# The last batch of an attention-and-experts layer: VectorE sums the fourth tile's experts, ScalarE scales the last expert, the output leaves in three pieces

## The chip, the cores and the metric

The kernel runs on one core of one Trainium2 chip. Its time is device microseconds, start to end of one execution. The engines are TensorE (PE, its weight loads PEld), VectorE (DVE), ScalarE (ACT), GpSimd (POOL) and SyncE (SP), which only issues transfers here.

## What is computed

The input x is 8 x 512 x 128. It is normalised to xn, and the output is x plus an attention of xn plus a mixture of 8 experts of which each token takes its best two. Masked scores are set to 0, not to minus infinity.

```
def attention(x, Wq, Wk, Wv):            # per batch, T = 512, width 128
    q, k, v = x @ Wq.T, x @ Wk.T, x @ Wv.T
    attn = (q @ k.T) * tril(ones(T, T))
    return softmax(attn / sqrt(T)) @ v

def experts(x, Wg, We, be):              # E = 8, tokens t
    gates = softmax(x @ Wg)
    top_g, top_i = top_k(gates, 2); top_g /= sum(top_g)
    dispatch[e, t] = top_g where e in top_i[t], else 0
    return sum_e dispatch[e, t] * (x[t] @ We[e] + be[e])

xn = layernorm(x)
out = x + attention(xn, Wq, Wk, Wv) + experts(xn, Wg, We, be)
```

## The kernel before

The 512 tokens of a batch are four tiles of 128. The batches 0 to 7 go through a pipeline that is written out by hand: each engine has one list of calls, in program order, and semaphores order the engines against each other. An engine does its calls in the order written, so a call that waits holds all that stand behind it. The last batch, B - 1 = 7, and the end of batch 6 have lists of their own, behind the loop.

TensorE, for each tile t of batch b:

- `wide(b, k, t)` multiplies xn by a group of weights: C (values, expert 7, gate logits; 264 columns), A (four experts, 512 columns) and B (three experts, 384 columns). Each is three matmuls, of a high and a low part (L239, L240, L243), into one of four PSUM banks, the ring. `ring_free` lets it start only when the use of the group four places before it in the list of groups is over. In the last batch these are: B0 waits for A3 of batch 6, A1 for `sv_rows`, A2 for ScalarE's scaling of A0, B2 for the mix of tile 0, B3 for the scaling of A1, A3 for the mix of tile 1, and the row transpose DT for the scaling of A2.
- `scores(b, t)` writes the scores of the tile (t + 1) * 128 columns wide to one of three banks; `transpose_probs(b, t)` (L277) turns the exponentials, t + 1 blocks; `attend(b, t)` (L293) multiplies them with the values into the bank attb, 2 (t + 1) matmul records in the trace.
- `value_sums` (SV) and `transpose_rows` (DT, L328) prepare one low-rank matmul, `bias` (L334), which adds the masked keys' part and the experts' biases to all four tiles of attb. It ends the batch on TensorE.

VectorE: the gate (maxima, sum, reciprocal, `gate_out`, L528), `sv_rows` (L608), the masking of scores with their maximum (`mask_scores`, L560) and its negation `negate_max` (nmx, L567), `mix_b(b, t, i)` (L543), which adds gate times expert for the three experts of group B to x, the softmax sums (`softmax_sum`, `softmax_tot`, `softmax_rec`), and `finish_tile(b, t)` (L597), which scales attb and adds ffn into o_s.

ScalarE: copies out of PSUM, `softmax_exp` (L840), `probs_copy` (L855), and `scale_experts(b, t)` (L829), four multiplications of group A's experts by their gates into ysc. `rows_copy` (L886) lies between DT and the bias.

GpSimd: `scale_last(b)` (L1003) multiplies expert 7 of all four tiles by its gate, into y7. `sum_experts(b, t)` (L1010 to L1017) is a chain of four additions: the four scaled experts, y7, and the mix, into ffn. `bias_rows(b)` (L1029 to L1041) builds the rows for DT out of the gates and softmax totals.

SyncE stores batches 0 to 6 whole. The last batch goes in two pieces: tiles 0 to 2 when they are finished, then tile 3.

## Time and profile before

| | us |
|---|---|
| median of 3 runs | 132.51 (130.95 to 132.6) |
| the profiled execution's own time | 132.71 |
| its span in the profile | 130.69 |
| TensorE busy | 121.3 |
| VectorE / ScalarE / GpSimd busy | 102.1 / 101.4 / 96.2 |

The span is what the trace shows, from the first to the last event; 2.0 us lie around it. All times of the trace are counted from the start of the span. A busy TensorE is not TensorE at its peak, since matmuls overlap: in a timeline the record of one lasts longer than the step to the next. The start times in the chain of work are the better measure of what one costs.

### The profile page before, as it was taken

The numbers are of one execution on the slowest core, as the hardware profiler recorded it, in microseconds if no ns is written. First come the engines' busy times: TensorE is split into PE (matmuls) and PEld (weight loads), VectorE is DVE, ScalarE is ACT, GpSimd is POOL, SyncE is SP. The second block draws the span as 40 slices with busy tenths as digits, with TensorE's granted clock in tenths as the row PEclk, the third lists the DMA queues.
The fourth block names the chain that finished last, engine by engine and source line by source line (L and its number), as shares of the span: only waits on it lengthen the run. The fifth ranks groups of instructions, "written<-read, shape, count | busy, mean of one in ns | idle before, by whom it ended". The sixth has DMA issues, their size and how long they took to land.

```text
span 130.7 us, 3014 instructions
## 1 busy us (share of the span) xinstructions
PE 121.3 (93%) x766; PEld 109.1 (83%) x766; DVE 102.1 (78%) x507; ACT 101.4 (78%) x341; POOL 96.2 (74%) x216
## 2 busy tenths in 40 slices
PE   4839999999999999999999999999999999999870
PEld 4717878998989989999899999999899899888650
DVE  0477789797988799697969796979877985967822
ACT  2145699979986999789996999699869999656850
POOL 7080228669995998689967997799859986788881
PEclk9999999999999999999999999999999999999999
DMA  2996000000020002000200020000200020002002
GB/s 65 362 295 164 0 0 8 0 3 3 10 70 5 3 0 80 0 0 3 82 3 3 0 78 10 0 0 7 78 5 0 0 80 0 0 5 83 3 0 80
DMA packets 8929, 5.18 MB, mean 40 GB/s; under 512 B 328, under 2 KB 8784, under 8 KB 8912
## 3 DMA queue, kind: packets, MB, share of 16 engines
q1 hardware_dynamic: 8608, 4.79, 12.5%
q10 hardware_dynamic: 304, 0.20, 0.5%
q8 instruction: 6, 0.10, 0.3%
q14 instruction: 11, 0.09, 0.2%
HBM read 2.89 MB, written 2.10 MB: 38 GB/s over the span
## 4 chain that ended last, share of the span: by engine, by line
PE 83%; DVE 7%; DMA 3%; POOL 2%; ACT 1%; issue 1%; POOLq 0%
PE ring L239 13%; PE ring L240 13%; PE ring L243 13%; PE attb L293 12%; PE score L277 6%; PE ring L320 4%; PE score L243 4%; PE score L240 4%; PE score L239 3%; DMA x_all<-in_x_dram 3%; PE ring L302 2%; PE ring L310 2%; PE ring L313 2%; PE ring L311 2%; DVE xn L648 2%; PE ring L328 1%
## 5 line engine op out<-in xcount | busy, mean ns | idle before, releaser
L829 ACT ACTIVATE ysc<-ring,gate 128x128 f32<-128x128 f32 x128 | 36.4, 372 | 3.4 <-DVE gate L528 1.5
L239 PE MATMUL ring<-w_hi,xT_hi 128*128 128x264 f32 (+2 forms) x96 | 35.2, 367 | 0.6 <-DVE mix L543 0.4
L240 PE MATMUL ring<-w_lo,xT_hi 128*128 128x264 f32 (+2 forms) x96 | 33.0, 344 | 0.0
L243 PE MATMUL ring<-w_hi,xT_lo 128*128 128x264 f32 (+2 forms) x96 | 32.9, 343 | 0.0
L1010 POOL TENSOR_TENSOR ysc<-ysc 128x256 f32<-128x256 f32 x32 | 23.5, 734 | 7.3 <-ACT ysc L829 7.3
L293 PE MATMUL attb<-c_s,probT 128*128 128x128 f32 x160 | 23.3, 278 | 0.0
L543 DVE SCALAR_TENSOR_TENSOR mix<-ring,gate,mix 128x128 f32<-128x128 f32 x64 | 22.0, 344 | 0.2
L239 PEld LDWEIGHTS ring<-w_hi,xT_hi 128*128 128x128 f32 x96 | 18.7, 194 | 3.3 <-DVE mix L543 0.6
L293 PEld LDWEIGHTS attb<-c_s,probT 128*128 128x128 f32 x160 | 20.8, 191 | 0.4
L240 PEld LDWEIGHTS ring<-w_lo,xT_hi 128*128 128x128 f32 x96 | 18.6, 194 | 1.6
L243 PEld LDWEIGHTS ring<-w_hi,xT_lo 128*128 128x128 f32 x96 | 18.5, 193 | 1.4
L1017 POOL TENSOR_TENSOR ffn<-ysc,mix 128x128 f32<-128x128 f32 x32 | 14.6, 457 | 6.5 <-DVE tot L582 4.3
L840 ACT ACTIVATE prob<-score,nmx 128x128 f32<-128x128 f32 (+3 forms) x32 | 17.4, 542 | 0.6 <-DVE nmx L567 0.6
L543 DVE SCALAR_TENSOR_TENSOR mix<-ring,gate,x_all 128x128 f32<-128x128 f32 x32 | 11.0, 345 | 7.9 <-PE ring L243 7.7
L597 DVE SCALAR_TENSOR_TENSOR o_s<-attb,rinv,ffn 128x128 f32<-128x128 f32 x32 | 10.8, 344 | 8.0 <-PE attb L334 7.9
L1013 POOL TENSOR_TENSOR ysc<-ysc,y 128x128 f32<-128x128 f32 x32 | 14.7, 461 | 2.5
L1011 POOL TENSOR_TENSOR ysc<-ysc 128x128 f32<-128x128 f32 x32 | 14.7, 459 | 2.5
L560 DVE CUSTOM_DVE_ANT_0 score<-score,causal 128x128 f32<-128x128 f32 (+3 forms) x32 | 15.7, 490 | 0.1
L990 POOL TENSOR_TENSOR rstd<-veps,half 128x4 f32<-128x4 f32 x8 | 8.1, 1014 | 9.5 <-DVE veps L475 5.9
L277 PE MATMUL score<-ident,prob 128*128 128x128 f32 x80 | 14.2, 276 | 0.2 <-ACT prob L840 0.2
L855 ACT COPY probT<-score 128x128 f32<-128x128 f32 (+3 forms) x32 | 13.8, 430 | 0.4 <-PE score L277 0.3
L801 ACT ACTIVATE xn<-x_all,nmr,rstd 128x128 f32<-128x128 f32 x29 | 12.0, 483 | 1.6 <-POOL nmr L998 1.6
(99 smaller groups left out, 248.9 us busy)
## 6 DMA issues: line engine op xcount, KB each, us to landing
x_all<-in_x_dram SPq DMA_DIRECT2D x8, 256.0 KB, 5.9
out_dram<-o_s SPq DMA_DIRECT2D x7, 256.0 KB, 2.3
w_f<-in_w_stacked_dram SPq DMA_DIRECT2D x1, 580.0 KB, 5.2
out_dram<-o_s SPq DMA_DIRECT2D x1, 192.0 KB, 2.1
wqk_s<-in_w_attention_dram ACTq DMA_DIRECT2D x1, 128.0 KB, 3.7
shapes_s<-in_shapes_dram ACTq DMA_DIRECT2D x1, 64.5 KB
out_dram<-o_s SPq DMA_DIRECT2D x1, 64.0 KB, 1.8
be_s<-in_be_dram ACTq DMA_DIRECT2D x1, 4.0 KB
```

Of the source, the lines that this page charges most:

```text
L239: nc.tensor.matmul(dst, hi, w_h, start=True, stop=False)
L240: nc.tensor.matmul(dst, hi, w_l, start=False, stop=False)
L243: return nc.tensor.matmul(dst, lo, w_h, start=False, stop=True)
L277: last = nc.tensor.transpose(score_bank(b, t)[:, c], prob[:, t, c], ident[:])
L293: last = nc.tensor.matmul(attb[:, t * P:(t + 1) * P], probT[:, b % 2, t, j * P:(j + 1) * P], c_s[:, b % 2, j, 0:P], start=(t == 0), stop=F ...
L543: ins = nc.vector.scalar_tensor_tensor(mix[:, t, i, :], bank(f"B{t}", b)[:, i * P:(i + 1) * P], gate[:, b % 2, t, 4 + i:5 + i], before, AL ...
L560: cnt["maxed", b, t] = chain.mark(nc.vector.tensor_tensor_reduce(score_bank(b, t)[:, 0:n], score_bank(b, t)[:, 0:n], causal[:, (NT - 1 - t ...
L829: last = nc.scalar.mul(ysc[:, t, e, :], bank(f"A{t}", b)[:, e * P:(e + 1) * P], gate[:, b % 2, t, e:e + 1])
L840: nc.scalar.activation(prob[:, t, 0:n], score_bank(b, t)[:, 0:n], ACT.Exp, bias=nmx[:, b % 2, t:t + 1], scale=1.0, accum_out=rs[:, b % 2, ...
L1010: chain.step(nc.gpsimd.tensor_tensor(y[:, 0:2, :], y[:, 0:2, :], y[:, 2:4, :], ALU.add))
L1011: chain.step(nc.gpsimd.tensor_tensor(y[:, 0, :], y[:, 0, :], y[:, 1, :], ALU.add))
L1013: chain.step(nc.gpsimd.tensor_tensor(y[:, 0, :], y[:, 0, :], y7[:, b % 2, t, :], ALU.add))
```

## The change

Only the end of batch 6 and the last batch are touched; the loops before are the same.

- `scale_last(B - 1)` on GpSimd is replaced by `scale_last_act(B - 1)` on ScalarE: three multiplications, for tiles 0 to 2.
- `scale_experts(B - 1, 3)` on ScalarE and `sum_experts(B - 1, 3)` on GpSimd go. VectorE does the same sum for tile 3 in a chain: four `mix_a` read group A's experts straight from PSUM, `mix_last` adds expert 7, and `finish_last` takes the place of `finish_tile(B - 1, 3)`.
- The orders of the calls on TensorE, VectorE, ScalarE and GpSimd are rewritten.
- The last batch is stored in three pieces: tiles 0 and 1, tile 3, tile 2. The finishes come in the order 0, 1, 3, 2.

```diff
@@ SyncE
+            b = B - 1
+            sp.wait_ge(S["fin_done"], b * NT + 2)
+            sp.dma_start(out_v[b][:, 0:2, :], o_s[:, b % 2, 0:2, :]).then_inc(S[f"stored{b % 2}"], 16)
+            for n, t in enumerate((3, 2)):
+                sp.wait_ge(S["fin_done"], b * NT + 3 + n)
+                sp.dma_start(out_v[b][:, t, :], o_s[:, b % 2, t, :]).then_inc(S["stored_last"], 16)
+            sp.wait_ge(S["stored_last"], 32)
@@ TensorE
             transpose_probs(B - 1, 0)
+            scores(B - 1, 2)
             wide(B - 1, "B", 0)
-            scores(B - 1, 2)
             wide(B - 1, "A", 1)
+            scores(B - 1, 3)
             wide(B - 1, "B", 1)
-            scores(B - 1, 3)
+            transpose_probs(B - 1, 1)
             wide(B - 1, "A", 2)
             wide(B - 1, "B", 2)
+            transpose_probs(B - 1, 2)
+            attend(B - 1, 0)
             wide(B - 1, "B", 3)
-            transpose_probs(B - 1, 1)
-            wide(B - 1, "A", 3)
-            attend(B - 1, 0)
-            transpose_probs(B - 1, 2)
             transpose_probs(B - 1, 3)
             attend(B - 1, 1)
+            wide(B - 1, "A", 3)
             attend(B - 1, 2)
@@ VectorE
+            def mix_a(e):
+                b, t = B - 1, NT - 1
+                if e == 0:
+                    dve.wait_ge(S["wide_done"], wide_count("A", b, t))
+                    dve.wait_ge(S["mix_ready"], b * NT + t + 1)
+                else:
+                    chain.need(cnt["mix_a", e - 1])
+                cnt["mix_a", e] = chain.mark(nc.vector.scalar_tensor_tensor(
+                    mix[:, t, e % 2, :], bank(f"A{t}", b)[:, e * P:(e + 1) * P], gate[:, b % 2, t, e:e + 1],
+                    mix[:, t, 2 if e == 0 else 1 - e % 2, :], ALU.mult, ALU.add))
+
+            def mix_last():
+                b, t = B - 1, NT - 1
+                chain.need(cnt["mix_a", 3])
+                cnt["mix_last"] = chain.mark(nc.vector.scalar_tensor_tensor(
+                    mix[:, t, 0, :], c_s[:, b % 2, t, Y_AT:Y_AT + P], gate[:, b % 2, t, 7:8], mix[:, t, 1, :], ALU.mult, ALU.add))
+
+            def finish_last(b):
+                t = NT - 1
+                chain.need(cnt["mix_last"])
+                nc.vector.scalar_tensor_tensor(o_s[:, b % 2, t, :], attb[:, t * P:(t + 1) * P], rinv[:, b % 2, t:t + 1],
+                                               mix[:, t, 0, :], ALU.mult, ALU.add).then_inc(S["fin_done"], 1)
...
             negate_max(B - 1, 1)
+            gate_out(B - 1)
             finish_tile(B - 2, 0)
-            gate_out(B - 1)
...
+            for e in range(4):
+                mix_a(e)
+            mix_last()
             finish_tile(B - 1, 0)
             finish_tile(B - 1, 1)
+            finish_last(B - 1)
             finish_tile(B - 1, 2)
-            finish_tile(B - 1, 3)
@@ ScalarE
+            def scale_last_act(b):
+                act.wait_ge(S["gate_ready"], b + 1)
+                act.wait_ge(S["ffn_ready"], (b - 2) * NT + NT)
+                for t in range(NT - 1):
+                    last = nc.scalar.mul(y7[:, b % 2, t, :], c_s[:, b % 2, t, Y_AT:Y_AT + P], gate[:, b % 2, t, 7:8])
+                last.then_inc(S["y7_ready"], 1)
...
             sv_high(B - 1)
+            scale_last_act(B - 1)
+            softmax_exp(B - 1, 1)
+            probs_copy(B - 1, 0)
             scale_experts(B - 1, 0)
-            probs_copy(B - 1, 0)
-            softmax_exp(B - 1, 1)
+            softmax_exp(B - 1, 2)
             scale_experts(B - 1, 1)
-            scale_experts(B - 1, 2)
             probs_copy(B - 1, 1)
-            softmax_exp(B - 1, 2)
             masked_exp(B - 1)
             softmax_exp(B - 1, 3)
             probs_copy(B - 1, 2)
+            scale_experts(B - 1, 2)
             probs_copy(B - 1, 3)
-            scale_experts(B - 1, 3)
@@ GpSimd
             sum_experts(B - 2, 3)
-            scale_last(B - 1)
             sum_experts(B - 1, 0)
             sum_experts(B - 1, 1)
+            bias_rows(B - 1)
             sum_experts(B - 1, 2)
-            bias_rows(B - 1)
-            sum_experts(B - 1, 3)
```

Three places show the new order. Line numbers below 540 on TensorE move by one and those of VectorE by one or 27, since functions are added.

VectorE at the last gate, before. grec is the reciprocal of the gate sums, nmx the negated maximum of tile 1, the o_s rows are the finishes of batch 6, the rhs_rows are `sv_rows`.

```order
L517 RECIPROCAL grec<-gsum 128x4
L543 SCALAR_TENSOR_TENSOR mix<-ring3,gate,mix 128x128
L567 TENSOR_SCALAR nmx<-mx 128x1
L597 SCALAR_TENSOR_TENSOR o_s<-attb,rinv,ffn 128x128
L528 TENSOR_TENSOR gate<-gexp,grec 128x32
L608 SCALAR_TENSOR_TENSOR rhs_rows<-sv_hi,shapes_s,ring1 3x128 x3
L543 SCALAR_TENSOR_TENSOR mix<-ring0,gate,x_all 128x128
L597 SCALAR_TENSOR_TENSOR o_s<-attb,rinv,ffn 128x128 x2
L543 SCALAR_TENSOR_TENSOR mix<-ring0,gate,mix 128x128
L597 SCALAR_TENSOR_TENSOR o_s<-attb,rinv,ffn 128x128
```

The same place now; L587 with 128x384 is the mask of tile 2.

```order
L518 RECIPROCAL grec<-gsum 128x4
L544 SCALAR_TENSOR_TENSOR mix<-ring3,gate,mix 128x128
L594 TENSOR_SCALAR nmx<-mx 128x1
L529 TENSOR_TENSOR gate<-gexp,grec 128x32
L624 SCALAR_TENSOR_TENSOR o_s<-attb,rinv,ffn 128x128
L635 SCALAR_TENSOR_TENSOR rhs_rows<-sv_hi,shapes_s,ring1 3x128 x3
L624 SCALAR_TENSOR_TENSOR o_s<-attb,rinv,ffn 128x128
L587 ISA score0,mx<-score0,causal 128x384
L587 ISA mx 128x1
L624 SCALAR_TENSOR_TENSOR o_s<-attb,rinv,ffn 128x128
L594 TENSOR_SCALAR nmx<-mx 128x1
L624 SCALAR_TENSOR_TENSOR o_s<-attb,rinv,ffn 128x128
```

The gate has passed the first finish of batch 6, and the mask of tile 2 has passed the mixes of tile 0.

TensorE around group A3 of the last batch (bank ring2, 512 columns), before. score2, score0 and score1 hold tiles 1, 2 and 3; the attb rows are `attend`.

```order
L277 MATMUL score2<-ident,prob 128x128 x2
L239 MATMUL ring2<-w_hi,xT_hi 128x512
L240 MATMUL ring2<-w_lo,xT_hi 128x512
L243 MATMUL ring2<-w_hi,xT_lo 128x512
L293 MATMUL attb<-c_s,probT 128x128
L277 MATMUL score0<-ident,prob 128x128 x3
L277 MATMUL score1<-ident,prob 128x128 x4
L293 MATMUL attb<-c_s,probT 128x128 x9
```

The same place now; ring1 with 384 columns is group B3.

```order
L278 MATMUL score0<-ident,prob 128x128 x3
L294 MATMUL attb<-c_s,probT 128x128
L240 MATMUL ring1<-w_hi,xT_hi 128x384
L241 MATMUL ring1<-w_lo,xT_hi 128x384
L244 MATMUL ring1<-w_hi,xT_lo 128x384
L278 MATMUL score1<-ident,prob 128x128 x4
L294 MATMUL attb<-c_s,probT 128x128 x2
L240 MATMUL ring2<-w_hi,xT_hi 128x512
L241 MATMUL ring2<-w_lo,xT_hi 128x512
L244 MATMUL ring2<-w_hi,xT_lo 128x512
L294 MATMUL attb<-c_s,probT 128x128 x7
```

All transposes and two of the `attend` calls now stand ahead of A3, seven matmuls of `attend` behind it.

VectorE at the end, before: the softmax totals of the last batch, the mixes of tile 3 (ring1) and the four finishes.

```order
L582 TENSOR_TENSOR tot<-tot,rs 128x4
L586 RECIPROCAL rinv<-tot 128x4
L543 SCALAR_TENSOR_TENSOR mix<-ring1,gate,mix 128x128 x2
L597 SCALAR_TENSOR_TENSOR o_s<-attb,rinv,ffn 128x128 x4
```

The end now: L559 is `mix_a`, L567 `mix_last`, L574 `finish_last`.

```order
L609 TENSOR_TENSOR tot<-tot,rs 128x4
L544 SCALAR_TENSOR_TENSOR mix<-ring1,gate,x_all 128x128
L613 RECIPROCAL rinv<-tot 128x4
L544 SCALAR_TENSOR_TENSOR mix<-ring1,gate,mix 128x128 x2
L559 SCALAR_TENSOR_TENSOR mix<-ring2,gate,mix 128x128 x4
L567 SCALAR_TENSOR_TENSOR mix<-c_s,gate,mix 128x128
L624 SCALAR_TENSOR_TENSOR o_s<-attb,rinv,ffn 128x128 x2
L574 SCALAR_TENSOR_TENSOR o_s<-attb,rinv,mix 128x128
L624 SCALAR_TENSOR_TENSOR o_s<-attb,rinv,ffn 128x128
```

Five chained instructions have come in ahead of the finishes, and tile 3's finish stands third.

## Rows read from the trace of the kernel before

**Rows 1.** The page: busy time by engine; a group: busy us, mean ns of one | idle before.

```profile
PE 121.3 (93%) x766; PEld 109.1 (83%) x766; DVE 102.1 (78%) x507; ACT 101.4 (78%) x341; POOL 96.2 (74%) x216
...
L855 ACT COPY probT<-score 128x128 f32<-128x128 f32 (+3 forms) x32 | 13.8, 430 | 0.4 <-PE score L277 0.3
```

**Rows 2.** The chain in order of time, last batch: start us, us, what.

```profile
115.39 0.23 PE ring L239
...
118.14 0.17 PE ring L239
...
118.66 0.23 PE score L239
...
119.35 0.23 PE ring L239
...
120.05 0.17 PE ring L239
...
122.56 0.79 ACT prob L840 x2
```

**Rows 3.** Timeline of TensorE: start us, us, engine, line, what, [idle before <-releaser].

```profile
121.72 0.50 PE L239 MATMUL ring<-w_hi,xT_hi 128*128 128x512 f32 x1 [0.40 <-DVE mix L543]
...
123.88 2.17 PE L293 MATMUL attb<-c_s,probT 128*128 128x128 f32 x18
```

**Rows 4.** Timeline of VectorE.

```profile
113.93 0.18 DVE L517 RECIPROCAL grec<-gsum 128x4 f32<-128x4 f32 x1
...
115.43 0.35 DVE L597 SCALAR_TENSOR_TENSOR o_s<-attb,rinv,ffn 128x128 f32<-128x128 f32 x1 [1.02 <-PE attb L334]
115.70 0.46 DVE L528 TENSOR_TENSOR gate<-gexp,grec 128x32 f32<-128x32 f32 x1
116.08 1.05 DVE L608 SCALAR_TENSOR_TENSOR rhs_rows<-sv_hi,shapes_s,ring 3x128 fp32r<-3x128 f32 x3
...
119.22 0.56 DVE L560 CUSTOM_DVE_ANT_0 score<-score,causal 128x384 f32<-128x384 f32 x1
...
120.94 0.73 DVE L543 SCALAR_TENSOR_TENSOR mix<-ring,gate,mix 128x128 f32<-128x128 f32 x2
121.58 0.69 DVE L560 CUSTOM_DVE_ANT_0 score<-score,causal 128x512 f32<-128x512 f32 x1
...
127.12 0.87 DVE L597 SCALAR_TENSOR_TENSOR o_s<-attb,rinv,ffn 128x128 f32<-128x128 f32 x3 [2.25 <-PE attb L334]
128.15 0.35 DVE L597 SCALAR_TENSOR_TENSOR o_s<-attb,rinv,ffn 128x128 f32<-128x128 f32 x1 [0.15 <-POOL ffn L1017]
```

**Rows 5.** Timeline of ScalarE.

```profile
100.90 1.65 ACT L801 ACTIVATE xn<-x_all,nmr,rstd 128x128 f32<-128x128 f32 x4 [0.18 <-POOL nmr L998]
...
116.22 1.14 ACT L829 ACTIVATE ysc<-ring,gate 128x128 f32<-128x128 f32 x4 [1.48 <-DVE gate L528]
```

**Rows 6.** Timeline of GpSimd.

```profile
115.65 0.45 POOL L1017 TENSOR_TENSOR ffn<-ysc,mix 128x128 f32<-128x128 f32 x1
116.23 1.05 POOL L1003 TENSOR_TENSOR y<-c_s,gate 128x512 f32<-128x512 f32 x1
...
124.51 0.23 POOL L1029 TENSOR_TENSOR gate_tot<-gate,tot 128x32 f32<-128x32 f32 x1
...
125.30 0.25 POOL L1041 TENSOR_TENSOR lhs_rows<-gate_tot,lhs_rows 128x32 fp32r<-128x32 f32 x1
125.78 0.72 POOL L1010 TENSOR_TENSOR ysc<-ysc 128x256 f32<-128x256 f32 x1 [0.23 <-ACT ysc L829]
...
127.66 0.45 POOL L1017 TENSOR_TENSOR ffn<-ysc,mix 128x128 f32<-128x128 f32 x1
```

**Rows 7.** Timeline of SyncE's queue: the two stores of the last batch.

```profile
128.02 0.37 SPq L214 DMA_DIRECT2D out_dram<-o_s  x1
128.52 0.40 SPq L216 DMA_DIRECT2D out_dram<-o_s  x1
```

More of the change, by code:

```diff
@@ L210, in _ @@
                 store(b)
-            b, t = B - 1, NT - 1
-            sp.wait_ge(S["fin_done"], b * NT + t)
-            sp.dma_start(out_v[b][:, 0:t, :], o_s[:, b % 2, 0:t, :]).then_inc(S[f"stored{b % 2}"], 16)
-            sp.wait_ge(S["fin_done"], b * NT + NT)
-            sp.dma_start(out_v[b][:, t, :], o_s[:, b % 2, t, :]).then_inc(S["stored_last"], 16)
-            sp.wait_ge(S["stored_last"], 16)
+            b = B - 1
[5 more added lines that the diff above has]
+            sp.wait_ge(S["stored_last"], 32)
             for i in range(2):
@@ L759, in _ @@
             sv_rows(B - 1, 2)
+            finish_tile(B - 2, 1)
+            mask_scores(B - 1, 2)
+            finish_tile(B - 2, 2)
+            negate_max(B - 1, 2)
+            finish_tile(B - 2, 3)
             mix_b(B - 1, 0, 0)
-            finish_tile(B - 2, 1)
-            finish_tile(B - 2, 2)
             mix_b(B - 1, 0, 1)
-            finish_tile(B - 2, 3)
+            mix_b(B - 1, 0, 2)
+            mask_scores(B - 1, 3)
             mix_b(B - 1, 1, 0)
-            mix_b(B - 1, 0, 2)
-            mask_scores(B - 1, 2)
+            negate_max(B - 1, 3)
+            mix_b(B - 1, 1, 1)
             mix_b(B - 1, 2, 0)
-            negate_max(B - 1, 2)
-            mix_b(B - 1, 1, 1)
             mix_b(B - 1, 1, 2)
-            mask_scores(B - 1, 3)
-            negate_max(B - 1, 3)
-            mix_b(B - 1, 3, 0)
             mix_b(B - 1, 2, 1)
@@ L778, in _ @@
             softmax_tot(B - 1)
+            mix_b(B - 1, 3, 0)
             softmax_rec(B - 1)
```

## The prediction

> **What bounds the kernel now.** I read the page first: TensorE is busy 93% of the span, 121.3 us [rows 1]. That is an average over eight batches, and the change touches only the last one, so the views that decide are the chain and the timelines from 115 us on. Nothing is moved ahead of the last gate, about 114.3 us, so the first 114 us should repeat.
>
> In the chain [rows 2], take the differences of the start times: `wide(B)` 384 columns costs 0.52 us (118.14 to 118.66), `scores` of tile 3 0.69, `wide(A)` 0.70. The tail of attention, 18 multiplications in 2.17 us [rows 3], gives (2.17 - 0.27)/17 = 0.11 us for each 128-column one; probability transposes go at the same pace. TensorE's work between the end of the bias of batch 6 (115.39, where A0 begins, [rows 2]) and the end of the last `attend` (123.88 + 2.17 = 126.05, [rows 3]) is then 4 x 0.70 + 4 x 0.52 + 0.52 + 0.69 + 10 x 0.11 + 20 x 0.11 = 9.4 us; I carry 9.45, since the steps are rounded, and the dates below add to that. The stretch lasts 10.66. So **TensorE stands still for 1.2 us** there; the largest piece is A3 (121.72), which waits 0.40 for VectorE's mix of tile 1 [rows 3]. The chain shows why: VectorE's mix waits for B2, the mask of tile 3 (0.69 us) comes behind it at 121.58, and ScalarE's exponential of tile 3 only at 122.56 [rows 2, 4].
>
> After TensorE comes a fixed tail: row transpose, copy, bias, and the first `finish_tile` at 127.12, that is 1.07 us behind the last `attend`; then four finishes, the last held until 128.15 by GpSimd's `ffn` of tile 3 (done 127.66 + 0.45), and the last store issued at 128.52 [rows 3, 4, 6, 7]. The span ends 130.69 - 128.52 = 2.17 us later.
>
> **The change part by part.**
>
> *Gate ahead of finish_tile(6,0).* The reciprocal of the gate sum ends at 114.11, but the gate stood behind a finish that waited 1.02 us for TensorE, and came out at 115.70 + 0.46 = 116.16 [rows 4]. Now it can start at about 114.4 and takes 0.18 (its median in the other batches) to 0.46 us: ready at 114.6 to 114.9, 1.3 to 1.5 us earlier. ScalarE waited 1.48 us for exactly this [rows 5]. Its own new waits are for things of batch 5 and 6 that are long done. The three `sv_rows` start right behind the finish, 115.70 instead of 116.08, and so end at 116.78: A1, at 117.27 in the new flow, does not wait for them.
>
> *GpSimd loses `scale_last` (1.05 us) and `sum_experts(7,3)` (125.78 to 128.11, 2.33 us) [rows 6].* ScalarE gains three multiplications that read SBUF. The nearest rows are xn from SBUF, four in 1.65 us, about 0.40 each in a row [rows 5], and ysc from PSUM, four in 1.14, about 0.26 each. So 0.8 to 1.2 us; I take 1.2, since SBUF is the source. They run 114.64 to 115.84, in time in which ScalarE waited; the exponential of tile 1 (at most the 0.79 of tile 3, [rows 2]) ends by 116.6, and TensorE asks for it only at 119.20. It loses one `scale_experts` (1.14). Cost on the path: nothing; were the cover gone, 1.2 us.
>
> *VectorE gains four chained `mix_a` and one `mix_last`.* A pair of chained mixes takes 0.73 [rows 4], 0.36 each: 4 x 0.36 = 1.45. `mix_last` reads two SBUF tensors. The row to look at is the gate at 115.70: 0.46 us instead of 0.18, ending at 116.16, just behind GpSimd's `ffn` (115.65 + 0.45 = 116.10) [rows 4, 6]. So it costs 0.35 alone and up to 0.35 + 0.45 = 0.80 beside GpSimd; I take 0.8, since `sum_experts(7,2)` runs then. [...]
>
> *The new order, followed through.* TensorE from 115.39, no stalls: A0 to 116.10, transpose 0 to 116.21, scores 2 to 116.74, B0 to 117.27, A1 to 117.97, scores 3 to 118.67, B1 to 119.20, transposes 1 to 119.42, A2 to 120.12, B2 to 120.65, transposes 2 to 120.98, attend 0 to 121.20, B3 to 121.73, transposes 3 to 122.17, attend 1 to 122.61, A3 to 123.31, attend 2 to 123.98, attend 3 to 124.85. VectorE: sv_rows to 116.78, finish 1, mask 2 from 117.04 (0.56, [rows 4]), finish 2, negate (nmx 2 at 117.91), finish 3, mix 0 from 118.10 to 119.16, mask 3 from 119.09 to 119.84 with its read-out, nmx 3 at 120.1 instead of just ahead of 122.56, then mix 1 and mix 2 interleaved: mix 1 ready at 121.30, behind the first part of mix 2, which waits for B2 (120.65). ScalarE: scale 0 116.44 to 117.55, exp 2 from 117.94 to 118.7 at most, scale 1 to 119.6, copy 1 to 119.9, exp 3 from 120.15 to 120.9 (0.79 with the read-out of its sum, [rows 2]), copies by the mean of 0.43 [rows 1] and tile 3's somewhat longer: copy 2 from 121.0 to 121.5, scale 2 to 122.5, copy 3 from 122.4 to 123.0.
>
> Each wait of TensorE against its date: B2 needs mix 0 (119.18 for 120.12), A3 needs mix 1 (121.30 for 122.61), transposes 3 need exp 3 (120.9 for 121.73), attend 3 needs copy 3 (123.0 for 123.98), the row transpose needs `rows_ready`. For that GpSimd waits for tot: exp 3 at 120.9, then VectorE's softmax_sum and softmax_tot at about 122.3 with both delayed by GpSimd; the five operations of `bias_rows` take 124.51 to 125.55, 1.04 us [rows 6], so 123.35 for 124.85. The smallest slack is **0.8 us**. Then 1.2 us of stalls go, and the last `attend` ends at 124.85 instead of 126.05: **-1.20**.
>
> *The tail.* First finish 1.07 later, 125.91. VectorE must be done by then: A3 ends 123.31, mix_a 123.42 to 124.87, mix_last to 125.65 at the dear end: 0.25 us in hand. `sum_experts(7,2)` starts at 123.5 and takes 2.33: 125.83, wanted at 126.69 by the last finish. The finishes start every 0.26 us (three in 0.87, [rows 4]): 125.91, 126.17, 126.43 (tile 3), 126.69 (tile 2). The three pieces queue on SP: the first is issued when tile 1 ends, 126.55; an issue takes 0.37 and 0.40 in [rows 7], and I put 0.05 between two (at most the 0.13 between those): second 126.97, third 127.42. Its data (tile 2, done 127.04) is ready by then, so SP's own queue is what comes last. Before, the last issue began 1.40 behind the first finish (127.12 to 128.52), now 1.51: **+0.11**. The last piece is again 64 KB, so I keep 2.17 us from issue to the end.
>
> Sum: -1.20 + 0.11 = **-1.1 us**; span 129.6. The profiled execution took 132.71, so 131.6; it lies 0.2 above the median of 132.51, and against that median I get **131.4 us**.
>
> **Rivals.**
> 1. *A wait comes back at about half price.* Slacks are 0.8 to 1.5 us, but VectorE is in order and the chain mix 0, B2, mix 2, mix 1, A3 goes twice between engines; and mix_last has 0.25 us in hand. For: two of these slacks rest on what VectorE does in a row. Against: 0.8 us is more than the roundings of the steps on the way. A stall of 0.3 to 0.7: 131.9.
> 2. *Gains beyond the sum.* The third piece could be issued as soon as its tile is done (127.07, 0.35 earlier) if issues overlap, and the end could hang on a smaller queue. The issues of [rows 7] do not overlap, which speaks against it: 131.0.
> 3. *The end was set by GpSimd and the stores, and stays.* Then only 0.15 us of the wait for `ffn` goes and the 0.11 comes: 132.4. The chain runs through GpSimd at the end [rows 6], but TensorE's bias comes only 1 us before, so both ends move.
> 4. *Slower: VectorE becomes the bound at the end.* Place: A3, four chained mix_a, mix_last, then finish_tile(7,0) behind them. A3 begins 0.9 later than before (121.72, now 122.61), and 1.45 + 0.8 + 0.1 us of VectorE work that used to be ScalarE's and GpSimd's stands in front of all the finishes. The price is one for one from the moment that A3 ends later than 123.55; the gain is gone when it ends later than 124.65, which a wait for mix 1 would do if that came at 123.95 instead of 121.30. At 0.5 us beyond: 133.0. Against: 2.6 us of slip is more than any engine in this stretch shows.
> 5. *mix_last waits for GpSimd's chain, not for one instruction of it.* The instructions of `sum_experts(7,2)` follow each other closely, its last ends at 125.83. Had mix_last to wait for all of them, it would end at 126.2, and the first finish would slip from 125.91 by 0.3: 131.7. Against: the gate at 115.70 waited out one `ffn` only.
>
> **How the numbers follow.** All stalls gone and tail as summed: 0.55, 131.1 to 131.8 by profile to median. Rival 1: 0.2. Rival 2: 0.08. Rival 3: 0.07. Rival 4: 0.05. Rival 5: 0.05. The three times of before spread from 130.95 to 132.6, so a median of after can sit 1.5 us lower than the sum by that alone, or 0.3 higher; low end 131.4 - 1.5 = 129.9, high end rival 3 and part of rival 4, 132.7. Two per cent of 132.51 is 2.65 us, about what a measurement of this kernel can tell from no change; faster by more than that needs 129.86 or less, which only a spread as that of before gives: 0.06. Slower by over 2%, 135.2, needs rival 4 at five times its price: 0.02. Within: 0.92.
>
> **What the new profile would show.** Right: gate at about 114.6 and no 1.48 us of idle ScalarE before the first scale; nmx of tile 3 near 120.1; no wait before A3 and transposes 3; last attend near 124.9; first finish near 125.9; three issues one after the other from 126.5; span 129.6. Wrong: A3 or B2 with an idle time that ends with VectorE; the first finish released by VectorE's own mix and not by the bias; the last store waiting for a finish; a later issue than 127.5. The forecast falls if the old stalls reappear at the new places of the transposes, or if the last 64 KB land more slowly behind two fresh pieces.

## The result, and the profile after

| | before | changed |
|---|---|---|
| median of 20 runs, us | 132.64 (130.95 to 133.32) | 131.39 (130.34 to 132.03) |
| ratio, with 95% interval | | 0.9929 (0.9899 to 0.9958) |
| profiled execution: time, span, us | 132.71, 130.69 | 131.18, 129.11 |

The kernel became faster by 0.7%, and the interval of the ratio leaves 1 out; by ratio that is 0.9 us, by medians 1.25. The ratios here and below leave out executions that took over 1.5% more than the fastest of the same kernel: that is four of the six of experiment e1, whose ratio so rests on two, and one of e8, the very one that was profiled.

The two profiled spans differ by 1.58 us, but not all of this is the change. The stream of instructions is the same up to the last gate, and yet batch 6's bias ends at 115.39 before and at 115.02 in the changed kernel. In a second profile of the very same changed kernel (experiment e12) it ends at 115.56. So I count every date behind that point, called T0 below, from it. Behind T0 the span takes 15.30 us before and 14.10 in both profiles of the changed kernel: **the change is worth 1.20 us there**.

The stretch table of the changed kernel, T0 to the end of the last `attend`, and from there to the end (columns: the stretch, its length, busy us and instructions of PE, PEld, DVE, ACT, POOL, granted clock, DMA share, GB/s):

The first row is the same stretch before; a row of the changed kernel for each of the two follows.

```profile
115.39:126.05 10.66, 10.11 (x61) 8.51 (x60) 7.99 (x29) 7.91 (x27) 9.18 (x21) 1.00 0.09 28
...
115.02:124.44 9.42, 9.42 (x61) 8.50 (x60) 8.83 (x32) 6.86 (x24) 7.02 (x17) 1.00 0.11 31
124.44:129.10 4.66, 0.58 (x3) 0.19 (x1) 1.77 (x6) 0.27 (x1) 0.91 (x2) 0.87 0.19 56
```

TensorE is busy in all of its 9.42 us, where the stretch took 10.66 before. By busy time it was idle for only 0.55 us of that, not 1.2: the record of a 512-column matmul lasts 0.39 us and the next starts 0.23 behind it, so the first part of every wait is covered by the record before it. The start times give the whole loss. Its timeline shows the places where the stalls used to be; a row without brackets at its end had no idle time ahead of it. It answers to [rows 3]:

```profile
121.14 0.60 PE L278 MATMUL score<-ident,prob 128*128 128x128 f32 x4
121.58 0.61 PE L294 MATMUL attb<-c_s,probT 128*128 128x128 f32 x4
121.95 0.48 PE L240 MATMUL ring<-w_hi,xT_hi 128*128 128x512 f32 x1
...
122.72 1.72 PE L294 MATMUL attb<-c_s,probT 128*128 128x128 f32 x14
124.28 0.27 PE L329 MATMUL ring<-ident,lhs_rows 128*128 128x128 f32 x1
125.00 0.47 PE L335 MATMUL attb<-rhs_rows,lhsT_rows 128*128 128x512 f32 x1 [0.45 <-ACT lhsT_rows L924]
```

VectorE, against [rows 4]: the gate ends at 114.19, ahead of T0; the negated maximum of tile 3 comes at 119.62, T0 + 4.6, where it was T0 + 7.0; then the new sum.

```profile
113.96 0.23 DVE L529 TENSOR_TENSOR gate<-gexp,grec 128x32 f32<-128x32 f32 x1
...
119.62 0.14 DVE L594 TENSOR_SCALAR nmx<-mx 128x1 f32<-128x1 f32 x1
...
123.08 1.51 DVE L559 SCALAR_TENSOR_TENSOR mix<-ring,gate,mix 128x128 f32<-128x128 f32 x4
124.62 0.50 DVE L567 SCALAR_TENSOR_TENSOR mix<-c_s,gate,mix 128x128 f32<-128x128 f32 x1
125.50 0.61 DVE L624 SCALAR_TENSOR_TENSOR o_s<-attb,rinv,ffn 128x128 f32<-128x128 f32 x2 [0.39 <-POOL ffn L1055]
126.03 0.34 DVE L574 SCALAR_TENSOR_TENSOR o_s<-attb,rinv,mix 128x128 f32<-128x128 f32 x1
126.29 0.34 DVE L624 SCALAR_TENSOR_TENSOR o_s<-attb,rinv,ffn 128x128 f32<-128x128 f32 x1
```

Here is a trap. The row at 125.50 names GpSimd's `ffn` as what ended VectorE's wait, and the chain of waits follows it back through GpSimd:

```profile
124.52 0.45 POOL ysc L1051
124.97 0.04 issue
125.01 0.51 POOLq L93
125.52 0.34 DVE o_s L624
```

But the first finish needs the bias (125.00 + 0.47 = 125.47) and the `ffn` of tile 0, which was long done. The `ffn` that ends at 125.51 is tile 2's, wanted by the last finish at 126.29. Two events came within 0.04 us, and the profile took the later. In e2's profile, where no edit touches this place, the same row names the bias. Which of them held the finish, experiment e9 decides.

GpSimd and SyncE, against [rows 6, 7]:

```profile
124.52 0.45 POOL L1051 TENSOR_TENSOR ysc<-ysc,y 128x128 f32<-128x128 f32 x1
125.05 0.46 POOL L1055 TENSOR_TENSOR ffn<-ysc,mix 128x128 f32<-128x128 f32 x1
```

```profile
126.14 0.37 SPq L214 DMA_DIRECT2D out_dram<-o_s  x1
126.56 0.96 SPq L217 DMA_DIRECT2D out_dram<-o_s  x2
```

The two issues from 126.56 take 0.47 and 0.45 us, so the last begins at 127.07, though its tile was done at 126.63.

### The profile page after: what moved, and what is told of

Read it like the earlier page. It is cut to its first block, busy times and chain, and to the rows that moved or that the text cites. A ratio compares the mean times of both kernels' runs of the same rounds, so it can differ in the third digit from the quotient of the medians.

```text
span 129.1 us, 3013 instructions
## 1 busy us (share of the span) xinstructions
PE 120.2 (93%) x766; PEld 108.9 (84%) x766; DVE 103.3 (80%) x512; ACT 101.1 (78%) x340; POOL 93.4 (72%) x211
## 4 chain that ended last, share of the span: by engine, by line
PE 84%; DVE 6%; DMA 3%; POOL 3%; issue 1%; POOLq 0%; DVEq 0%
PE ring L240 13%; PE ring L244 13%; PE ring L241 13%; PE attb L294 13%; PE score L278 6%; PE score L244 4%; PE score L241 4%; PE ring L321 4%; PE score L240 3%; DMA x_all<-in_x_dram 3%; PE ring L303 2%; PE ring L314 2%; PE ring L311 2%; PE ring L312 2%; PE ring L329 1%; PE attb L335 1%
## 5 line engine op out<-in xcount | busy, mean ns | idle before, releaser
L859 ACT ACTIVATE ysc<-ring,gate 128x128 f32<-128x128 f32 x124 | 35.4, 373 | 0.8 <-PE ring L244 0.3
L1048 POOL TENSOR_TENSOR ysc<-ysc 128x256 f32<-128x256 f32 x31 | 22.8, 735 | 8.4 <-ACT ysc L859 8.4
L587 DVE CUSTOM_DVE_ANT_0 score<-score,causal 128x128 f32<-128x128 f32 (+3 forms) x32 | 15.7, 491 | 0.7 <-PE score L244 0.6
```

The source lines that it names most:

```text
L587: cnt["maxed", b, t] = chain.mark(nc.vector.tensor_tensor_reduce(score_bank(b, t)[:, 0:n], score_bank(b, t)[:, 0:n], causal[:, (NT - 1 - t ...
L859: last = nc.scalar.mul(ysc[:, t, e, :], bank(f"A{t}", b)[:, e * P:(e + 1) * P], gate[:, b % 2, t, e:e + 1])
L1048: chain.step(nc.gpsimd.tensor_tensor(y[:, 0:2, :], y[:, 0:2, :], y[:, 2:4, :], ALU.add))
```

## The experiments

All are edits of the changed kernel, except e12, which is that kernel again. Each was run 6 to 12 times beside the kernel of before, whose median then was 132.34 to 132.42, and profiled once. Dates behind T0, us, from each kernel's profile:

| kernel | nmx, tile 3 | last attend ends | first finish starts | last finish ends | end of span | median | ratio to before (95%) |
|---|---|---|---|---|---|---|---|
| before | 7.0 | 10.66 | 11.73 | 13.11 | 15.30 | 132.64 | 1 |
| changed | 4.6 | 9.43 | 10.49 | 11.62 | 14.10 | 131.39 | 0.993 (0.990, 0.996) |
| e12, the same again | 4.6 | 9.43 | 10.50 | 11.62 | 14.10 | 131.20 | 0.990 (0.985, 0.994) |
| e1 gate late | 5.0 | 9.61 | 10.68 | 11.92 | 14.28 | 131.87 | 0.989 (0.981, 0.997) |
| e2 two pieces | 4.6 | 9.43 | 10.50 | 11.63 | 13.87 | 130.50 | 0.988 (0.983, 0.992) |
| e3 tile 3 back | 4.6 | 9.41 | 10.48 | 13.13 | 15.10 | 132.33 | 0.999 (0.996, 1.002) |
| e4 old TensorE order | 4.9 | 10.66 | 11.72 | 12.84 | 15.31 | 132.92 | 1.003 (1.001, 1.006) |
| e5 y7 on GpSimd | 4.6 | 9.43 | 10.50 | 11.62 | 14.10 | 131.17 | 0.991 (0.987, 0.995) |
| e6 three more mixes | 4.6 | 9.42 | 11.03 | 12.15 | 14.63 | 132.21 | 0.999 (0.996, 1.002) |
| e7 store from ScalarE | 4.6 | 9.44 | 10.50 | 11.63 | 13.83 | 131.44 | 0.992 (0.989, 0.996) |
| e8 old VectorE order | 7.1 | 13.51 | 14.58 | 15.70 | 18.19 | 134.22 | 1.012 (1.008, 1.017) |
| e9 rows early | 4.6 | 9.55 | 10.02 | 11.14 | 13.61 | 130.53 | 0.986 (0.982, 0.989) |
| e10 rows early, two pieces | 4.6 | 9.54 | 10.01 | 11.13 | 13.37 | 130.72 | 0.988 (0.984, 0.991) |
| e11 sum moved alone | 7.0 | 10.67 | 11.74 | 12.86 | 15.34 | 132.44 | 1.001 (0.998, 1.004) |

The dates repeat to 0.01 or 0.02 us from profile to profile wherever nothing was edited; the times of whole runs scatter by 1.5 us, since T0 itself does (113.5 to 115.9). Differences of 0.2 us are therefore read from the dates alone.

**e1: the gate back behind the finish.**

```diff
-            gate_out(B - 1)
             finish_tile(B - 2, 0)
+            gate_out(B - 1)
```

> The changed kernel, with the last gate put back behind the first finish of batch 6; all else as changed. Theory (TensorE is now without stalls, and the early gate is one of the reasons): counted from the end of batch 6's bias (T0, 115.02 in the changed kernel's trace), the gate comes at T0 + 0.8 instead of before T0, ScalarE's three y7 multiplications move from before T0 to after it, so the copy of tile 0's transposed probabilities comes at about T0 + 2.7 and holds scores 3 by 0.3, the exponential of tile 3 ends at about T0 + 6.3 instead of 5.5 and holds the transposes of tile 3 by about 0.2: the last attend ends at T0 + 9.9 instead of 9.42, time +0.5 us (0.3 to 0.8). Rival (the early gate only fills ScalarE's idle time; all slack is larger): same last attend at T0 + 9.4, time 0.

Measured: +0.18, between the 0.5 of the theory and the 0 of the rival. The gate came at T0 + 0.77 as expected, but only A1 waited, for the later `sv_rows`:

```profile
115.06 0.33 PE L244 MATMUL ring<-w_hi,xT_lo 128*128 128x384 f32 x1
115.32 0.50 PE L240 MATMUL ring<-w_hi,xT_hi 128*128 128x512 f32 x1
```

From the start of the last matmul of B0 to the first of A1 it is 0.26 us, and from there to the second of A1 0.34 (115.66); in the changed kernel it was 0.17 and 0.23. The two differences, 0.2 us together, are the loss, and the kernel of before has the same steps there, 0.27 and 0.33. The slacks on ScalarE held, so the 0.3 and 0.2 that I expected at scores 3 and the transposes of tile 3 were not lost. Off TensorE more was lost than shows at the end: GpSimd's `ffn` of tile 2 ended at T0 + 11.54 instead of 10.49 and held the last finish by 0.1 us (it ends at 11.92 instead of 11.62), which SP's queue of issues then covered. Of the 1.2 us the early gate is worth 0.2 by these dates; by medians it would be 0.5 and by ratios nothing, both within the scatter.

**e2: two pieces.**

```diff
-            for n, t in enumerate((3, 2)):
-                sp.wait_ge(S["fin_done"], b * NT + 3 + n)
-                sp.dma_start(out_v[b][:, t, :], ...).then_inc(S["stored_last"], 16)
-            sp.wait_ge(S["stored_last"], 32)
+            sp.wait_ge(S["fin_done"], b * NT + 4)
+            sp.dma_start(out_v[b][:, 2:4, :], ...).then_inc(S["stored_last"], 16)
+            sp.wait_ge(S["stored_last"], 16)
```

> The changed kernel with the last batch stored in two pieces, tiles 0 and 1, then tiles 2 and 3 together when all is finished. Theory (SP's own queue of issues, 0.37 to 0.47 us each, comes last; the third is issued at 127.06, 0.43 after the last finish at 126.63): the last issue comes 0.40 us sooner, 1.16 behind the first finish instead of 1.56, and the time falls by 0.3 to 0.4 us. Rival (128 KB at the end land later than 64 KB, or the issue overlaps with the landing of the earlier ones): 0, or slower by 0.1 to 0.3.

Measured: -0.23 behind T0. The timeline of SyncE's queue:

```profile
126.42 0.37 SPq L214 DMA_DIRECT2D out_dram<-o_s  x1
126.94 0.37 SPq L216 DMA_DIRECT2D out_dram<-o_s  x1
```

T0 is 115.28 in this profile, so the last issue comes at T0 + 11.66 instead of 12.05, the expected 0.4 sooner. From there to the end of the span it is 2.21 us instead of 2.04. Each theory has its part: the queue did come last, and 0.17 of it comes back in the landing. The third piece costs more than it brings.

**e3: tile 3 back on ScalarE and GpSimd**, all orders new.

```diff
-            for e in range(4):
-                mix_a(e)
-            mix_last()
             finish_tile(B - 1, 0)
             finish_tile(B - 1, 1)
-            finish_last(B - 1)
             finish_tile(B - 1, 2)
+            finish_tile(B - 1, 3)
@@ ScalarE
             probs_copy(B - 1, 3)
+            scale_experts(B - 1, 3)
@@ GpSimd
             sum_experts(B - 1, 2)
+            sum_experts(B - 1, 3)
```

> The changed kernel with the experts of tile 3 back on ScalarE (four multiplications behind the last copy, and a fourth y7) and GpSimd (a chain of additions behind that of tile 2), finishes in the order 0, 1, 2, 3 and pieces (0, 1), 2, 3; all orders else as changed. Theory (the reordering takes the stalls out of TensorE, but only with the sum on VectorE does the end follow): last attend stays at T0 + 9.4, GpSimd's chain of tile 3 starts when that of tile 2 ends (T0 + 10.5) and takes 2.33, so the last finish starts at T0 + 12.9 instead of 11.3 and the last issue at T0 + 13.2 instead of 12.04: time +1.2 us, nearly the time of before. Rival (the stalls are all there is to the gain): 0 to +0.2.

Measured: +1.00 behind T0, ratio 0.999. TensorE kept all it had won (9.41), and the end did not move: VectorE stood 1.44 us before the last finish, until GpSimd's chain was through.

```profile
126.13 0.87 DVE L624 SCALAR_TENSOR_TENSOR o_s<-attb,rinv,ffn 128x128 f32<-128x128 f32 x3 [2.54 <-POOL ffn L1053]
128.43 0.35 DVE L624 SCALAR_TENSOR_TENSOR o_s<-attb,rinv,ffn 128x128 f32<-128x128 f32 x1 [1.44 <-POOL ffn L1053]
```

```profile
126.08 0.72 POOL L1046 TENSOR_TENSOR ysc<-ysc 128x256 f32<-128x256 f32 x1
...
127.95 0.45 POOL L1053 TENSOR_TENSOR ffn<-ysc,mix 128x128 f32<-128x128 f32 x1
```

**e4: TensorE's old order**, the others new.

```diff
             wide(B - 1, "B", 0)
+            scores(B - 1, 2)
             wide(B - 1, "A", 1)
             wide(B - 1, "B", 1)
+            scores(B - 1, 3)
             wide(B - 1, "A", 2)
             wide(B - 1, "B", 2)
             wide(B - 1, "B", 3)
+            transpose_probs(B - 1, 1)
+            wide(B - 1, "A", 3)
             attend(B - 1, 0)
+            transpose_probs(B - 1, 2)
             transpose_probs(B - 1, 3)
...
```

> The changed kernel with TensorE's order of the last batch as before the change (tile 1's transposes behind group B3, A3 before the first attend, all other transposes behind A3); the other engines as changed. Theory (TensorE's order has to fit the others'): ScalarE's copy of tile 1 stands ahead of the exponential of tile 3 and now waits for transposes that come at T0 + 5.8, so the exponential ends at about T0 + 6.9 and the copy of tile 3 at T0 + 9.1; the last attend waits some 0.5 for it and ends at T0 + 9.9 to 10.1: +0.6 us (0.3 to 0.9). Rival (the gain comes from VectorE's order alone): 0.

Measured: last attend 10.66 instead of 9.9 to 10.1, +1.21 behind T0: the theory's mechanism, at twice the size. ScalarE's copy of tile 1 waits 1.25 us for its transposes, the exponential of tile 3 stands behind it, and the copy of tile 3 comes late:

```profile
121.04 0.37 ACT L893 COPY probT<-score 128x256 f32<-128x256 f32 x1 [1.25 <-PE score L278]
121.31 0.21 ACT L886 ACTIVATE em<-nmx 128x3 f32<-128x3 f32 x1
121.42 0.68 ACT L878 ACTIVATE prob<-score,nmx 128x512 f32<-128x512 f32 x1
...
122.72 0.48 ACT L893 COPY probT<-score 128x384 f32<-128x384 f32 x1 [0.53 <-PE score L278]
```

```profile
121.17 0.51 PE L240 MATMUL ring<-w_hi,xT_hi 128*128 128x512 f32 x1 [0.16 <-DVE mix L544]
...
124.77 1.16 PE L294 MATMUL attb<-c_s,probT 128*128 128x128 f32 x8 [0.54 <-ACT probT L893]
```

ScalarE waited another 0.53 us for tile 2's transposes with the scaling of tile 2 queued behind, which I had not counted. That this doubled the loss is an argument from these rows; no run parts the two waits.

**e5: expert 7 scaled on GpSimd.**

```diff
             sum_experts(B - 2, 3)
+            scale_last(B - 1)
             sum_experts(B - 1, 0)
@@ ScalarE
-            scale_last_act(B - 1)
```

> The changed kernel with expert 7 scaled by GpSimd again (one multiplication of four tiles, 1.05 us, ahead of sum_experts of tile 0), and no y7 on ScalarE. Theory (both engines have room there): GpSimd does it from about T0 + 0.7 to T0 + 1.8, before ScalarE has tile 0's experts scaled at T0 + 2.2, so nothing on TensorE's path moves: last attend T0 + 9.4, time 0 (within 0.15). Rival (ScalarE was freed for the exponentials by nothing else, or GpSimd's queue is what the change relieves): the sums of all tiles and the softmax rows come 1.05 us later, and the time rises by 0.3 or more.

Measured: every date the same to 0.01 us. This part of the change is worth nothing, as GpSimd had 1.5 us of idle time there.

**e6: three more chained mixes.**

```diff
             for e in range(4):
                 mix_a(e)
+            for e in range(3):
+                chain.need(cnt["mix_a", 3])
+                mix_a(3)
             mix_last()
```

> The changed kernel with the fourth mix of tile 3 done four times over instead of once, with the same result: three more chained VectorE instructions of 0.37 us in front of the finishes. Theory (VectorE has about 0.4 us in hand: mix_last ends at 125.12, the first finish starts at 125.50 when the bias comes): of the 1.1 us, 0.4 are swallowed, the first finish starts 0.7 later, released by VectorE's own mix and not by the bias, time +0.7 us (0.5 to 0.8). Rival (VectorE is already the bound at the end): +1.1. Rival (GpSimd's sum of tile 2, done at 125.51, is what held the first finish): +0.7 too, but then with the first finish never earlier than the end of that sum in any run.

Measured: first finish +0.54, end +0.53. VectorE's timeline:

```profile
123.92 2.67 DVE L559 SCALAR_TENSOR_TENSOR mix<-ring,gate,mix 128x128 f32<-128x128 f32 x7
126.62 0.35 DVE L567 SCALAR_TENSOR_TENSOR mix<-c_s,gate,mix 128x128 f32<-128x128 f32 x1
126.89 0.60 DVE L624 SCALAR_TENSOR_TENSOR o_s<-attb,rinv,ffn 128x128 f32<-128x128 f32 x2
```

Three more cost 2.67 - 1.51 = 1.16 us, and about 0.6 was swallowed. `mix_last` now runs when GpSimd has finished for good (at T0 + 10.48; T0 is 115.86 here, so 126.34) and takes 0.35 instead of 0.50; that is the 0.15 by which the expected 0.7 was too much. The first finish no longer waits for anything but the instruction ahead of it.

**e7: tile 3's piece from ScalarE's queue.**

```diff
@@ ScalarE
             rows_copy(B - 1)
+            act.wait_ge(S["fin_done"], (B - 1) * NT + 3)
+            act.dma_start(out_v[B - 1][:, 3, :], ...).then_inc(S["stored_last"], 16)
```

SP keeps tiles 0 and 1, and tile 2 when all four are finished.

> The changed kernel with tile 3's piece issued from ScalarE's queue, which is idle at the end, and the other two from SP. Theory (SP's queue of issues is what comes last): the last issue from SP comes at the last finish, 126.66 instead of 127.06, with 64 KB to land, so the time falls by 0.3 to 0.4 us; beside the two-piece kernel this tells what the size of the last piece is worth. Rival (issues from two queues hinder each other, or the landing and not the issue counts): 0.

Measured: -0.27 behind T0; the ratio, 0.992, cannot tell it from the changed kernel. The last issue comes 0.39 sooner, as in e2, and here too the end follows it by more, 2.17 us instead of 2.04. So it is not the size of the last piece (64 or 128 KB, 0.04 us apart) that gives back the 0.13 to 0.17.

**e8: VectorE's old order** of masks, mixes and finishes, from `sv_rows` to the last mix of tile 3, with the early gate and the new sum.

```diff
             sv_rows(B - 1, 2)
-            finish_tile(B - 2, 1)
-            mask_scores(B - 1, 2)
...
+            mix_b(B - 1, 0, 0)
+            finish_tile(B - 2, 1)
+            finish_tile(B - 2, 2)
+            mix_b(B - 1, 0, 1)
+            finish_tile(B - 2, 3)
+            mix_b(B - 1, 1, 0)
+            mix_b(B - 1, 0, 2)
+            mask_scores(B - 1, 2)
+            mix_b(B - 1, 2, 0)
+            negate_max(B - 1, 2)
...
+            mask_scores(B - 1, 3)
+            negate_max(B - 1, 3)
```

> The changed kernel with VectorE's order of masks, mixes and finishes of batch 6 and 7 as before the change, but the early gate and the new sum of tile 3 kept. Theory (the mask of tile 3 ahead of the mixes of tiles 1 and 2 is what frees the exponential of tile 3, and with it TensorE's transposes): the mask of tile 3 stands behind a mix that waits for group B2 (T0 + 5.2), so nmx of tile 3 comes at about T0 + 7.0 instead of 4.7, the exponential ends at T0 + 8, and TensorE, which wants the transposes at T0 + 6.1 with A3 behind them, waits 1.8 us; the last attend ends at T0 + 11.2, A3 and VectorE's sum follow: +1.8 us, slower than the kernel of before. Rival (the order of VectorE is not what counts, since TensorE's new order alone gives the others time): 0 to +0.4.

Measured: slower than before, as expected by the theory, ratio 1.012. That is 2.5 us above the changed kernel's 0.993, or 3.0 above e12's 0.990, where the theory had 1.8. The profiled execution (135.61 us; the five others took 132.94 to 134.68) has its last attend at T0 + 13.5, 4.1 later than the changed kernel and 2.3 later than the 11.2 of the theory. The nmx of tile 3 came at T0 + 7.05 (expected 7.0), and TensorE's rows show waits of 1.21 + 0.26 + 0.25 us. By start times they cost more: the transposes of tile 3 start at T0 + 8.54 (123.90; T0 is 115.36), where it was T0 + 6.12, so **2.4 us are lost up to there**, 0.6 more than expected and close to what the ratios say. The other 1.7 us are in the rows behind that point:

```profile
121.83 0.55 PE L278 MATMUL score<-ident,prob 128*128 128x128 f32 x3 [1.21 <-ACT prob L878]
...
123.90 1.02 PE L278 MATMUL score<-ident,prob 128*128 128x128 f32 x4 [0.25 <-ACT prob L878]
124.72 1.06 PE L294 MATMUL attb<-c_s,probT 128*128 128x128 f32 x4
125.43 0.77 PE L240 MATMUL ring<-w_hi,xT_hi 128*128 128x512 f32 x1
126.00 0.63 PE L241 MATMUL ring<-w_lo,xT_hi 128*128 128x512 f32 x1
126.43 0.63 PE L244 MATMUL ring<-w_hi,xT_lo 128*128 128x512 f32 x1
```

Four transposes in 1.02 us instead of 0.60, and a step of 0.43 from one 512-column matmul to the next instead of 0.23. The stretch table shows a lower granted clock beside them (the column behind the five engines):

```profile
121.83:123.40 1.57, 1.31 (x8) 1.05 (x8) 0.70 (x3) 1.57 (x7) 0.51 (x1) 1.00 0.02 5
123.50:127.50 4.00, 3.75 (x16) 3.31 (x16) 2.20 (x10) 2.23 (x8) 3.63 (x11) 0.57 0.00 0
127.50:130.00 2.50, 1.95 (x14) 1.42 (x13) 1.45 (x5) 0.27 (x1) 0.91 (x2) 1.00 0.00 0
```

In those 4 us the granted clock was 0.57 in the mean. In steps of 0.25 us it reads 1.00 up to 124.00, 0.50 from 124.25 to 127.25, and 1.00 again from 127.50. TensorE had stood still for 1.21, 0.26 and 0.25 us before. The slowdown of e8 does not rest on this: another of its executions took 134.68 us with a granted clock of 0.998 in the mean of its whole span, so with hardly any time at a lowered clock. So e8 shows that VectorE's old order, beside TensorE's new one, costs more than the whole gain, but not that it costs 4.1 us.

**e9: the row transpose ahead of the last attend.**

```diff
-            attend(B - 1, 3)
             transpose_rows(B - 1)
+            attend(B - 1, 3)
```

> The changed kernel with TensorE's row transpose put ahead of the last attend, so that ScalarE's copy of it (0.27 us, with its waits 0.45 of idle TensorE) lies beside that attend. Theory (after the change the tail behind the last attend is what is left on TensorE's path, and VectorE has 0.4 us in hand, no more): the rows are ready at T0 + 8.2, the transpose is wanted at T0 + 8.5, the bias ends at about T0 + 9.8 instead of 10.46, but VectorE's mix_last ends only at T0 + 10.1, so the first finish starts at T0 + 10.05 to 10.1, released by VectorE itself: 0.4 us earlier, time -0.4. Rival (VectorE has more in hand than thought): -0.65. Rival (GpSimd's sum of tile 2, done at T0 + 10.5, holds the first finish): 0.

Measured: -0.49 behind T0, ratio 0.986. TensorE has no idle time any more, and the bias ends at T0 + 9.77; but the first finish starts only at T0 + 10.02 (124.44; T0 is 114.42), when VectorE is through with `mix_last` (the record of the finish starts 0.07 us ahead of the end of that of `mix_last`):

```profile
124.02 0.49 DVE L567 SCALAR_TENSOR_TENSOR mix<-c_s,gate,mix 128x128 f32<-128x128 f32 x1
124.44 0.60 DVE L624 SCALAR_TENSOR_TENSOR o_s<-attb,rinv,ffn 128x128 f32<-128x128 f32 x2
```

```profile
124.45 0.46 POOL L1055 TENSOR_TENSOR ffn<-ysc,mix 128x128 f32<-128x128 f32 x1
```

GpSimd's `ffn` of tile 2 starts only when the first finish does. So it never held the first finish, and the name in the changed kernel's row at 125.50 was a coincidence.

**e10: rows early and two pieces.**

```diff
-            attend(B - 1, 3)
             transpose_rows(B - 1)
+            attend(B - 1, 3)
@@ SyncE
-            for n, t in enumerate((3, 2)):
...
+            sp.wait_ge(S["fin_done"], b * NT + 4)
+            sp.dma_start(out_v[b][:, 2:4, :], ...).then_inc(S["stored_last"], 16)
```

> The row transpose ahead of the last attend, and the last batch stored in two pieces, tiles 0 and 1, then tiles 2 and 3. Theory: the gains add, -0.4 by the earlier finishes and -0.2 by the stores (the issue 0.4 sooner, 0.2 given back by the landing of 128 KB, as the two-piece kernel's trace has it), -0.6 us against the changed kernel; from the end of batch 6's bias to the end of the span 13.5 instead of 14.1. Rival (both shorten the same wait of SP's queue): no more than -0.4 together.

Measured: 13.37 behind T0, that is -0.73 against the changed kernel: the gains add. By the medians e9 (130.53) and e10 (130.72) cannot be told apart; by the dates e10 is 0.24 us shorter. Both beat both kernels.

**e11: the sum moved alone.** Every order as before, `scale_last` on GpSimd; only the new functions of VectorE, the order of the last finishes and the three pieces are kept. Against the kernel of before:

```diff
@@ VectorE
             mix_b(B - 1, 3, 2)
+            for e in range(4):
+                mix_a(e)
+            mix_last()
             finish_tile(B - 1, 0)
             finish_tile(B - 1, 1)
+            finish_last(B - 1)
             finish_tile(B - 1, 2)
-            finish_tile(B - 1, 3)
@@ ScalarE
-            scale_experts(B - 1, 3)
@@ GpSimd
-            sum_experts(B - 1, 3)
```

> The other half of the change by itself: the sum of tile 3 on VectorE, the finishes in the order 0, 1, 3, 2 and three pieces, but every order else as before the change, with the late gate and expert 7 scaled by GpSimd. Theory (the moved sum is worth nothing as long as TensorE's stalls stay): TensorE's last attend stays at T0 + 10.66, the first finish at T0 + 11.7; the wait for GpSimd at the fourth finish (0.15 us) goes, and the third piece costs SP 0.1 to 0.2: span behind T0 15.2 to 15.4, as before the change; time 0 against before. Rival (the end was set by GpSimd's chain of tile 3): -0.3 or more against before.

Measured: 15.34 behind T0 against 15.30, ratio 1.001. The stalls are those of before (0.40 ahead of A3, 0.16 ahead of the transposes of tile 3), and the sum on VectorE brings nothing.

**e12: the changed kernel again.**

> The changed kernel itself once more, as the measure for the three others on the same chip. All theories: ratio to before 0.991 to 0.994; span behind T0 14.1.

Measured: ratio 0.990, 14.10 behind T0, as expected.

## Why the prediction was right, by its own steps

*The stalls.* Predicted: last attend at T0 + 9.45, -1.20. Measured 9.43, -1.23. The method, adding the start-to-start steps of TensorE's groups and checking each wait against its date, gave the dates of the other engines too: nmx of tile 3 at T0 + 4.7 (measured 4.6), A3's mix in time, `rows_ready` at 123.22 for a transpose at 124.28. The smallest slack was nearer than the predicted 0.8 us: the exponential of tile 3 was read out at 120.57 for transposes that start at 121.14, 0.6.

*What made them go.* The prediction gave the reordering as a whole. The experiments split it: TensorE's new order and VectorE's are both needed (e4: +1.2 by dates, e8: +2.5 to 3.0 by ratios), the early gate is worth 0.2 of it (e1), and y7 on ScalarE nothing (e5). The prediction's "cost on the path: nothing" for y7 stands, but so would it have on GpSimd; the three multiplications took 0.99 us (114.25 to 115.24) instead of 1.2.

*The moved sum.* It cost VectorE 1.51 + 0.50 us; predicted 1.45 + 0.80. The 0.80 was the dear end of a bound and too dear, for two reasons that the rows show. GpSimd's instruction beside it had begun at 124.52, 0.1 ahead, and ended at 124.97; and `mix_last` ended 0.15 behind that, at 125.12, not a full 0.35. It came to 0.50 us beside GpSimd, and 0.35 in e6 without it. Rival 5 (mix_last waits for GpSimd's whole chain) is out: it ended at 125.12, GpSimd's chain at 125.51.

*The tail.* Predicted: +0.11 for SP's queue, and 2.17 us from the last issue to the end. Measured: +0.17, since an issue right behind another took 0.45 to 0.47 and not 0.40, and 2.04. Together +0.04 (0.17 - 0.13); the two misses cancel in part. The whole is -1.20 behind T0 against -1.1 predicted. That the median, 131.39, hits the 131.4 so closely is luck: executions scatter by 1.5 us with T0, the 132.51 that the prediction started from was a median of three where twenty give 132.64, and by ratio the gain is 0.9 us.

*The rivals.* Rival 1 (a wait comes back): no brackets in TensorE's timeline. Rival 2: the issues did not overlap (126.56 + 0.47 = 127.03, the next at 127.07). Rival 3 (GpSimd and the stores set the end anyway) is wrong for the changed kernel but right for half of the change: with the sum left on GpSimd, e3, the end stays at 15.10. The prediction named the moved sum only as a cost to VectorE and as a relief of GpSimd of 2.33 us; it did not say that without it the 1.2 us would have been lost. Rival 4 (VectorE as the bound) did not come, but is the next in line: e9 finds 0.47 us in hand (first finish at T0 + 10.02 instead of 10.49), and e6 uses them up. The prediction had 0.25, for its dear `mix_last`.

## What to carry to other kernels

Two changes that are each worth almost nothing can be worth the whole gain together. Here TensorE's stalls and GpSimd's last chain ended side by side: removing the stalls alone gave 0.2 us (e3), moving the chain alone lost 0.04 (e11), both gave 1.2. Before judging one edit by its own measurement, look how soon behind the removed wait the next one ends.

Hunt for the next bound by the same table of dates: one line moved on TensorE (e9) took another 0.5 us, as much as VectorE had in hand. And do not split the last store more often than its parts can be issued: a third piece held the queue for 0.4 us.

A releaser in a profile can be the latest event and not the awaited one, as `ffn` (125.51) was for the first finish at 125.50, behind the bias (125.47). When two come within 0.04 us of each other, an edit that moves only one of them decides.

## What the runs showed of the hardware

- In e8's profile TensorE's granted clock read 0.50 from 124.25 to 127.25 us (0.57 in the mean of 123.50 to 127.50) behind standstills of 1.21, 0.26 and 0.25 us, and 512-column matmuls then stepped by 0.43 instead of 0.23 us. In the kernel of before, with 0.40 and 0.15 of idle time in the same stretch, it stayed at 1.00. That the standstill made it fall was not tested, and it is one execution.
- An issue on SP's queue right behind another takes 0.44 to 0.47 us; one behind a pause takes 0.35 to 0.37. Before the change, 0.13 us behind the end of the one before, it took 0.40. From the end of the last issue to the end of the span it was 1.59 to 1.60 us in every kernel that issues three pieces from SP, in e3 too, where the last one came 1.17 us behind the one before it, and 1.77 to 1.85 in those with two pieces on SP (before, e2, e7, e10), for 64 and for 128 KB alike. So neither the size nor a pause makes the difference; what does is not shown. Counted from the start of the last issue to the end of the span it was 1.94 to 2.22 us over all these kernels.
- A VectorE instruction with two SBUF inputs (`mix_last`) took 0.49 to 0.50 us, and ended 0.14 to 0.15 behind the end of the GpSimd instruction beside it, in the seven profiles in which it began 0.10 to 0.12 us behind that one's start (changed, e2, e5, e7, e9, e10, e12). It took 0.35 where GpSimd was done or had at most 0.2 us of its instruction left (e1, e4, e6, e8, e11).
- In the first 115 us, which are the same code in all kernels up to the last gate, T0 varied from 113.5 to 115.9 us between executions; behind T0 the same code repeated to 0.02 us. All of the scatter arises early: the end of batch 0's bias comes between 29.8 and 32.1 us, and from there to T0 it is 83.6 to 83.8 us in every profile. What makes those first 30 us vary is not shown.
